# Two of the next group's query products moved from the tail of a token group into the last pairs of its attention, every tail step one product later

## The reference

```python
x = _layernorm(x + _L0_attn_ref(x, L0_attn_W_Q, L0_attn_W_K, L0_attn_W_V, L0_attn_W_O), axis=-1)
x = _layernorm(x + _L0_xattn_ref(x, ctx_1024, mask_BxSxS2_ik0, L0_xattn_W, L0_xattn_b), axis=-1)
x = _layernorm(x + _L0_ffn_ref(x, ...), axis=-1)      # top 2 of 8 experts
...                                                   # layer 1: attention, cross attention, ffn
```

## Time and profile before

| | us |
|---|---|
| median of three runs | 1233.13 |
| the profiled execution, its own time | 1236.84 |
| its span in the trace | 1235.1 |
| PE busy | 1099.2 (89%) |
| DVE busy | 725.8 (59%) |
| ACT busy | 543.2 (44%) |
| POOL busy | 461.5 (37%) |
| PE in the projections (L445), 384 records | 173.0 |
| first three attentions with their tails | from 53.6 to 397.7 |

### The profile page before, as it was taken

One profiled execution on the slowest core, in us unless ns is written; L12 is line 12 of the kernel. 1 busy time (PEld: TensorE's weight loads), 2 busy tenths in 40 slices (PEclk: granted clock), 3 DMA queues, 4 the chain that ended last, 5 costly groups with the idle time before them and its releaser, 6 DMA issues. The chain is left out here.

```text
span 1235.1 us, 20364 instructions
## 1 busy us (share of the span) xinstructions
PE 1099.2 (89%) x6750; PEld 793.1 (64%) x6750; DVE 725.8 (59%) x2212; ACT 543.2 (44%) x1379; POOL 461.5 (37%) x539
## 2 busy tenths in 40 slices
PE   7899989998999887799999948589898899899996
PEld 3476557545744676699999935355665575576874
DVE  1382366247525834456556547649849786966456
ACT  1381256227322821333333318357566657743551
POOL 0170034006300974566666635304522432323022
PEclk9999999999999998899999979679999999999999
DMA  6000200020002032651111114100100100000001
GB/s 202 18 2 1 59 18 2 0 58 19 1 0 59 2 113 73 242 178 53 44 53 50 46 52 145 35 1 1 35 9 1 35 10 18 1 2 26 1 1 35
DMA packets 40227, 52.38 MB, mean 42 GB/s; under 512 B 10780, under 2 KB 33372, under 8 KB 40124
## 3 DMA queue, kind: packets, MB, share of 16 engines
q1 hardware_dynamic: 31100, 36.66, 9.4%
q0 software_dynamic: 3408, 9.31, 2.7%
q10 hardware_dynamic: 5616, 5.11, 1.3%
HBM read 41.76 MB, written 9.31 MB: 41 GB/s over the span
## 5 line engine op out<-in xcount | busy, mean ns | idle before, releaser
L1682 PE MATMUL bank<-words 128*128 128x256 f32 (+3 forms) x872 | 266.9, 456 | 16.9 <-ACT words L2286 3.4
L1682 PEld LDWEIGHTS bank<-words 128*128 128x128 f32 (+1 forms) x872 | 162.1, 193 | 95.0 <-issue 56.1
L445 PE MATMUL bank<-words 128*128 128x512 f32 x384 | 173.0, 602 | 8.4 <-DMA words<-in_wq 8.4
L397 POOL TENSOR_TENSOR words<-words 128x256 f32<-128x256 f32 (+1 forms) x128 | 102.7, 833 | 155.2 <-DVE words L1016 154.7
L1219 PEld LDWEIGHTS bank<-words 128*128 128x128 f32 x1248 | 146.5, 193 | 3.5 <-ACT words L1253 1.6
L1219 PE MATMUL bank<-words 128*128 128x128 f32 x1248 | 147.0, 276 | 0.9 <-ACT words L1253 0.9
L445 PEld LDWEIGHTS bank<-words 128*128 128x128 f32 x384 | 72.5, 193 | 90.6 <-issue 90.3
L739 ACT ACTIVATE words<-words 128x128 f32<-128x128 f32 (+1 forms) x256 | 112.8, 444 | 30.6 <-DVE words L854 30.6
L731 ACT ACTIVATE words<-bank 128x512 f32<-128x512 f32 x48 | 28.7, 598 | 193.5 <-PE bank L445 193.5
L1268 ACT ACTIVATE words<-words 128x1024 f32 x39 | 41.1, 1057 | 144.3 <-PE bank L1219 112.8
L844 DVE COPY words<-bank 128x512 f32<-128x512 f32 x48 | 33.2, 691 | 106.7 <-PE bank L445 106.4
(11 more groups left out here) (346 smaller groups left out, 1983.7 us busy)
## 6 DMA issues: line engine op xcount, KB each, us to landing
words<-in_w SPq DMA_DIRECT2D x8, 1024.0 KB, 8.9
y_slots<-words ACTq DMA_DIRECT2D x39, 128.0 KB
words<-in_w SPq DMA_DIRECT2D x8, 512.0 KB, 9.4
words<-in_xt SPq DMA_DIRECT2D x4, 512.0 KB, 3.9
words<-in_x SPq DMA_DIRECT2D x4, 512.0 KB, 4.2
x_rows<-words SPq DMA_DIRECT2D x16, 128.0 KB, 1.8
words<-in_wm SPq DMA_DIRECT2D x2, 1024.0 KB, 6.7
out_x<-words SPq DMA_DIRECT2D x16, 128.0 KB, 1.8
```

The lines of the kernel that those rows point to most:

```text
L397: last = pool.tensor_tensor(part, part, inv[:, j % SLOTS0, :, t:t + 1].to_broadcast([P, 2, P * (t + 1)]), ALU.mult)
L445: last = pe.matmul(bank[c % 2][:, :], w, r, start=k == 0, stop=k == KD - 1)
L1682: last = pe.matmul(out, w, r, start=i == 0, stop=i == len(pairs) - 1)
```

## The change

Products 0 and 1 of the next group leave the tail. PE does product 0 at the end of turn 8 of the attention and product 1 at the end of turn 9. ACT takes product 0 out after its copy of turn 8, DVE takes product 1 out at its turn 10, behind the copies of the last transposed weights. The tail's loops begin at c = 2 on all three engines, and every step stands one number later. Each step of the tail so keeps as many products behind its predecessor as before, except that two products rather than three stand ahead of TURN1, and two rather than three behind COUNT.

```diff
+        AHEAD = 2
-        TURN1, QUERIES, LOGITS, TURNX, SUMS, TURN2, GATE = 3, 5, 7, 10, 12, 15, 17
-        CHOOSE, COUNT, RANK = 19, 21, 23
+        TURN1, QUERIES, LOGITS, TURNX, SUMS, TURN2, GATE = 4, 6, 8, 11, 13, 16, 18
+        CHOOSE, COUNT, RANK = 20, 22, 24
...
                     if turned_in(p):
                         units_turn(g, turned_in(p)[0])
+                    if g < FINAL and p in (TURNS - 3, TURNS - 2):
+                        project(g + 1, p - TURNS + 3)
...
-                for c in range(NCH + 1):
+                for c in range(AHEAD, NCH + 1):
...
-                    if c < NCH:
+                    if AHEAD <= c < NCH:
                         project(g + 1, c)
...
                     if 2 * p >= UNITS:
                         sums_copy(g, p)
+                    if g < FINAL and p == TURNS - 3:
+                        leave(g + 1, 0)
...
                         turned_copies(g, turned_in(p - 1)[0])
+                    if g < FINAL and p == TURNS - 1:
+                        leave(g + 1, 1)
```

## The result

The changed kernel takes 1241.24 us, the median of 18 runs (1236.77 to 1246.09), against 1231.96 for the kernel before beside it (18 runs): ratio 1.0078, 95% interval 1.0063 to 1.0093. It is 0.8%, 9.3 us, slower; forecast were 9.2.

The account below looks back on a forecast made before the run. PE was taken as the busiest engine, with no slack in the tail. Steps summed to 2.7 us in group 0 and 2.4 in the others, +7.5, plus 1.7 for the clock: +9.2 on 1233.13, 1242.3 us; range 1237.0 to 1248.0.

Parts of the forecast that it names:

- End of the attention: Before the output product: two moved products add 3.44 us, gaps cover 1.42, so it starts 2.0 us later per group.
- the rival on the falls at the starts: Clock falls at attention starts vanish or land in PE's waits, giving back 5.1 us: +2.4, 1235.5 us; chance 0.07.
- First norm: Two products, not three, precede its transposes, which come closer to the output product: -1.4, -1.7, -1.7 us by group.
- Parity: Copies preceding tail steps swap between ACT and DVE: norms' transposes -0.25 us each, attention weights' +0.4, together -0.1 a group.
- Product 15: Ahead of the second norm's transposes, product 15 waits for product 13's copy behind the norm: +2.2 us in each group.
- Rank: Tail's end: `rank` behind product 23's copy holds PE, cancelling the 1.72 us from one product fewer behind COUNT: 0.0.
- The clock: PE's clock falls behind the new 2.5 us gap at product 15, once in three tails: +1.7 us (0 to +5.1).

Follow-up runs that it names:

- rank late: The kernel before, with `rank` alone moved behind the copy of product 23 (RANK = 24): 1236.77 us, ratio 1.004.
- rank first: The change, but DVE ranks ahead of the copy of product 23 (RANK = 23): 1238.21 us, ratio to before 1.004.
- sums at 13: The kernel before, with SUMS at 13 and TURN2 at 16 alone, no moved product: 1241.58 us, ratio 1.0069.
- one product ahead: The kernel before, with product 0 alone moved to the end of turn 8, product 1 left in the tail, steps at their old numbers: 1227.43 us, ratio 0.996.

## Why the prediction was right

The time (1242.3 against 1241.2) and the sum (+9.2 against +9.3) were right, and so was the mechanism: the wait of product 15 is the bulk of the loss, and `rank` behind the last copy uses up what the shorter tail would give. That the sum met the median to 0.1 us is luck, since the interval of the ratio spans 7.8 to 11.5 us and two errors in it had opposite signs. By its steps, from the table above:

1. **End of the attention**, 2.0 forecast: 2.03 in group 0. In groups 1 and 2 it was 1.51 and 0.51. The difference is the rival on the falls at the starts, which came partly true: they didn't go away, but were moved by the 2.46 us gap to where PE waits. The experiment with rank late shows it in one attention without moved products (1.2 us of cost against 0.2 for the same fall). I had written this rival and the fall in a tail as alternatives; here both came, and the attentions cost 4.05 instead of 6.0.
2. **First norm**, -1.4, -1.7, -1.7 forecast: -1.44, -1.72, -1.73.
3. **Parity**, -0.1 a group forecast. Its three terms came nearly as sized, each by the distance to the next step's start: the first norm's transposes take 1.57 us instead of 1.73 (-0.16), the attention weights' 1.41 instead of 1.03 (+0.38), the second norm's 1.47 instead of 1.73 (-0.26). One was missed: the step LOGITS is now preceded by an odd product, whose copy keeps DVE from the first maximum, and PE waits for it between the logits. Timeline of group 0 after:

```profile
125.83 0.69 DVE L849 COPY words<-bank 128x512 f32<-128x512 f32 x1 [2.61 <-PE bank L446]
126.66 0.28 DVE L1048 CUSTOM_DVE_ANT_0 words<-bank,words 128x120 f32<-128x120 f32 x1
127.00 1.15 PE L512 MATMUL bank<-words 128*128 128x120 f32 x8 [0.32 <-DVE words L1048]
```

   The view of the logits' line after:

```profile
L512 PE MATMUL bank<-words x48: 264/275/370, 125.6 to 363.4; 128*128 128x120 f32 x48
its engine sat idle before it (us, times) until:
  DVE words L1048: 2.9, 6
  issue: 1.4, 6
```

   and before, where no wait for DVE stands:

```profile
L511 PE MATMUL bank<-words x48: 264/275/370, 126.5 to 359.0; 128*128 128x120 f32 x48
its engine sat idle before it (us, times) until:
  issue: 1.4, 6
```

   The logits take 2.36 us (125.63 to 127.99) against 1.97, +0.39 a group, 1.2 in all. So parity is +0.35 a group, inside its bounds.
4. **Product 15**, +2.2 forecast: from the sums' start to the second norm's transposes it is 148.65 - 138.01 = 10.64 against 8.51, +2.13. Sized right, and its cause is shown twice, by taking it out and by making it in the kernel before.
5. **Rank**, 0.0 forecast: the last stretch is 0.36 shorter, of which the norm's transposes are 0.26, so -0.1. The wait was 2.46, forecast 2.5, and hiding it gives back 1.63 a group, of which the attentions may keep some.
6. **The clock**, one fall of 1.7 in three tails forecast. The window of the change in group 1 that begins 0.27 us behind the gap's end:

```profile
264.00:268.00 4.00, 3.86 (x9) 1.58 (x9) 0.69 (x1) 0.57 (x2) 0.00 (x0) 0.57 0.66 207
```

   The fall costs 36.16 - 34.87 = 1.3 us before the second norm's transposes and 0.4 behind them, 1.7 together. The first profiled execution had one tail with a fall, the second two. The gap is what brings them: of the 15 tails with this gap (the change and rank first twice each, sums at 13 once) nine have a fall, which begins at most 1.3 us behind the gap's end; of the 21 tails of the other kernels none has. The Trainium skill (TensorE: Matmul & The Clock Gate, section "HAM oscillation") has as its abstract rule a limit on the idle gaps of PE that this gap does not reach. Read as the length below which the clock is safe, it does not hold here: the gap is 2.30 us, and 0.57 follows.

Summed over the trace, 4.05 - 4.89 + 9.42 - 0.69 = 7.9; the forecast was 6.0 - 4.8 + 8.75 (with step 6) - 0.75 = 9.2. In the second execution of the change it is 354.32 - 344.08 = 10.2: there the attentions cost 4.8 and the norm stretches, with two falls, 10.8. So two errors were partly balanced: the attentions were taken 2 us too dear, the logits' 1.2 were missing, a term that step 3 had left out although the product before LOGITS changes its parity as the others do.

What stays open: by the ratio, one product ahead gained 5 us, its touched stretch 3.3; the interval of the ratio (0.25% to 0.55%) reaches down to 3.1, so the two may agree. Whether the falls of the clock come as often in all executions as in the profiled ones, no run shows.

## What to carry to other kernels

Where two engines take alternate buffers and a table of numbers sets what stands between, and you shift a step by an odd number, its neighbour on each engine changes. Write down for each step which copy stands behind it in the same iteration, and which later product needs that copy. A filler moved into a gap gains the gap it fills, 1.4 of 3.44 us here, and that was worth 4 to 5 us; two waits made by the renumbering cost 12 to 14. If a step ends with a long chain through another engine, put the short copy that others wait for into the chain's wait, where it was free here.

## What the runs showed of the hardware

Falls of TensorE's clock that each lost 1.7 us of it made an attention 0 to 0.7 us longer when they came in its first 1.4 us, where PE waits for other engines, and 1.1 to 1.3 us longer when they came 7.5 to 8 us in. An idle gap of PE of 2.3 us, between two products (3.6 us) ahead and dense work behind, was followed by a fall in three of six tails of the change, and in nine of the 15 tails of this study that have it; without the gap the clock fell in none of 21 tails.
